# Normalising the attention input on ScalarE instead of VectorE, and all query projections ahead of all key projections

## The reference, cut to what matters

```python
x = x + layernorm(attn(layernorm(x), Mq, Mk, Mv))
x = x + layernorm(ffn(layernorm(x), w_gate, w_up, w_down))

def attn(x, Mq, Mk, Mv):        # x: 2048 x 1024 per batch, 8 heads of 64
    q = x @ Mq; k = x @ Mk; v = x @ Mv       # 512, 512, 1024 wide
    ...                                       # softmax over scores, times v
```

## Time and profile before

| what | value |
|---|---|
| median of 8 runs | 2291.67 us (2288.68 to 2415.04) |
| the profiled execution | 2290.75 us |
| its span on the slowest core | 2289.2 us |
| TensorE matmul busy | 1911.4 us (83%) |
| VectorE busy | 780.6 us (34%) |
| ScalarE busy | 872.8 us (38%) |

### The profile page before, as it was taken

The page is one execution under the profiler, slowest core; times in us unless marked ns, Lnnn a source line. Parts: engine busy times, 40 slices in busy tenths (PEclk is TensorE's granted clock), DMA queues, the critical chain, the costliest instruction groups (busy, mean ns, idle before and its releaser), DMA issues. The chain is left out here.

```text
span 2289.2 us, 35866 instructions; the slowest of 8 cores (2280.0 to 2289.2 us)
## 1 busy us (share of the span) xinstructions
PE 1911.4 (83%) x12864; PEld 1044.9 (46%) x12864; DVE 780.6 (34%) x1657; ACT 872.8 (38%) x1528; POOL 187.1 (8%) x150
## 2 busy tenths in 40 slices
PE   2967888886779995999956798888868999779997
PEld 1423565664435442444423345656644444334443
DVE  6123555656222213112125125556562121231211
ACT  2102888875422212211113128878753111131111
POOL 0011000101101011000110000001010000200002
PEclk7989798897789997999977897998987999979999
DMA  7097000000766404121041300000005220112201
GB/s 183 8 161 127 2 2 1 2 2 6 151 158 134 106 38 147 56 74 56 32 127 26 74 1 1 2 1 2 2 7 178 74 74 19 62 68 74 74 19 56
DMA packets 84553, 136.53 MB, mean 60 GB/s; under 512 B 29088, under 2 KB 33184, under 8 KB 84384
## 3 DMA queue, kind: packets, MB, share of 16 engines
q1 hardware_dynamic: 67744, 106.97, 14.6%
q0 software_dynamic: 16640, 27.27, 8.5%
HBM read 121.63 MB, written 35.65 MB: 69 GB/s over the span
## 5 line engine op out<-in xcount | busy, mean ns | idle before, releaser
L579 ACT ACTIVATE att<-S 128x1024 bf16<-128x1024 f32 x512 | 518.9, 1022 | 112.9 <-PE S L500 111.4
L842 PE MATMUL psG<-x2T,wgT 128*128 128x512 bf16 x1536 | 369.9, 384 | 16.4 <-ACT hT L862 16.4
L853 PE MATMUL psU<-x2T,wuT 128*128 128x512 bf16 x1536 | 363.9, 380 | 0.0
L893 PE MATMUL psD<-wdT,hT 128*128 128x512 bf16 x1536 | 332.2, 379 | 5.8 <-PEq L57 5.8
L865 DVE TENSOR_TENSOR hT<-hT,psU 128x512 bf16<-128x512 bf16 x192 | 132.0, 688 | 531.5 <-PE psU L853 518.0
L862 ACT ACTIVATE hT<-psG 128x512 bf16<-128x512 f32 x192 | 114.8, 598 | 491.8 <-PE psG L842 491.7
L461 PE MATMUL O<-v,att 128*128 128x128 bf16 x4096 | 284.6, 229 | 0.0
L461 PEld LDWEIGHTS O<-v,att 128*128 128x128 bf16 x4096 | 248.4, 103 | 48.4 <-issue 48.4
L842 PEld LDWEIGHTS psG<-x2T,wgT 128*128 128x128 bf16 x1536 | 150.8, 99 | 196.0 <-issue 24.2
L893 PEld LDWEIGHTS psD<-wdT,hT 128*128 128x128 bf16 x1536 | 150.0, 98 | 188.0 <-issue 7.7
L853 PEld LDWEIGHTS psU<-x2T,wuT 128*128 128x128 bf16 x1536 | 150.7, 98 | 183.0 <-issue 3.1
(11 more groups left out here) (81 smaller groups left out, 1053.3 us busy)
## 6 DMA issues: line engine op xcount, KB each, us to landing
wgT<-wgT_scratch SPq DMA_DIRECT2D x36, 512.0 KB, 3.5
wuT<-wuT_scratch SPq DMA_DIRECT2D x36, 512.0 KB, 4.3
x_sb<-x SPq DMA_DIRECT2D x8, 2048.0 KB, 11.9
out<-x_sb SPq DMA_DIRECT2D x32, 512.0 KB, 2.6
wdT<-wdT_scratch SPq DMA_DIRECT2D x2, 6144.0 KB, 35.4
xn_stage<-wd POOLq DMA_DIRECT2D x24, 256.0 KB, 5.2
wdT_scratch<-wks SPq DMA_DIRECT2D x24, 256.0 KB, 5.5
wgst<-wg POOLq DMA_DIRECT2D x24, 256.0 KB, 5.0
```

The costliest lines, as they stand in the source:

```text
L579: S.add("scalar", lambda sc, K=K, att_out=att_out, sl6=sl6, c=c: sc.activation(att_out, Sp[K % 2][:, :], AF.Exp, scale=0.125, accum_out=ac ...
L842: S.add("tensor", lambda tt, wsl=wsl, wcol=wcol, dt=dt, gsl=gsl, c2=c2: tt.matmul(psG[gsl][:, :], wgT_s[wsl][:, wcol + 128 * dt:wcol + 128 ...
L853: S.add("tensor", lambda tt, wsl=wsl, wcol=wcol, dt=dt, gsl=gsl, c2=c2: tt.matmul(psU[gsl][:, :], wuT_s[wsl][:, wcol + 128 * dt:wcol + 128 ...
L893: S.add("tensor", lambda tt, slot=slot, tau=tau, d2h=d2h, ht=ht, Sc=Sc: tt.matmul(psD[slot][tau][:, 512 * d2h:512 * (d2h + 1)], hT[:, 1024 ...
```

## The change

The first layer norm's per-tile operation moves from VectorE to ScalarE, as an Identity activation with a bias and a scale for each partition. The bias is now minus mean times reciprocal root, so the small VectorE operation ahead of it becomes two. Within a tile the order on ScalarE is: normalisation, then the copy of the same tile's transposes. The q and k groups are reordered: 16 q groups, then 16 k groups, in each the four row blocks for one quarter of columns. The first half of Mv is loaded after group 16 and the second after group 32, and each quarter of k is copied to `kTs` as soon as its four groups are evacuated.

```diff
-            negm_done = S.add("vector", lambda v, g4=g4, mean_v4=mean_v4: v.tensor_scalar(
-                nmr1[:, 4 * g4:4 * g4 + 4], mean_v4, -1.0, None, AL.mult),
+            nm1_done = S.add("vector", lambda v, g4=g4, mean_v4=mean_v4: v.tensor_tensor(
+                nmr1[:, 4 * g4:4 * g4 + 4], mean_v4, rstd1[:, 4 * g4:4 * g4 + 4], AL.mult),
                 waits=[(c_act, rstd_done)], inc=c_dve)
+            negm_done = S.add("vector", lambda v, g4=g4: v.tensor_scalar(
+                nmr1[:, 4 * g4:4 * g4 + 4], nmr1[:, 4 * g4:4 * g4 + 4], -1.0, None, AL.mult),
+                waits=[(c_dve, nm1_done)], inc=c_dve)
             for t in tiles:
-                S.add("vector", lambda v, t=t: v.tensor_scalar(
+                S.add("scalar", lambda sc, t=t: sc.activation(
                     xn_bf[:, D * (t % 2):D * (t % 2 + 1)], x_sb[:, D * t:D * (t + 1)],
-                    nmr1[:, t:t + 1], rstd1[:, t:t + 1], AL.add, AL.mult),
+                    AF.Identity, bias=nmr1[:, t:t + 1], scale=rstd1[:, t:t + 1]),
                     waits=[(c_dve, negm_done), (s_tp, tp_base + t - 1)], inc=s_xn)
...
-        for c in range(4):
-            for q in range(4):
+        for q in range(4):
+            for c in range(4):
                 proj_groups.append(("q", q, c))
-            for q in range(4):
+        for q in range(4):
+            for c in range(4):
                 proj_groups.append(("k", q, c))
...
-                        waits=[(s_proj, proj_base + 28 + 4 * half)],
+                        waits=[(s_proj, proj_base + 16 * (half + 1))],
...
-                lastg = 28 + i1
-                if lastg % 2 == 0:
-                    kw = [(s_evP, evP_base + lastg // 2 + 1)]
-                else:
-                    kw = [(s_evPA, evPA_base + (lastg + 1) // 2)]
+                kw = [(s_evP, evP_base + 10 + 2 * i1), (s_evPA, evPA_base + 10 + 2 * i1)]
```

## The result

The changed kernel takes 2331.68 us (median of 11 runs, 2326.86 to 2591.07) against 2291.72 us of the kernel before on the same chip (31 runs). The ratio is 1.0173, interval 1.0154 to 1.0192: slower, inside the forecast range. The profiled execution took 2327.58 us (span 2325.9), 36.8 us more than that of before; the sum had said 2323.9. The mean granted clock lies between 0.904 and 0.907 on all eight cores.

The account below looks back on a forecast made before the run. VectorE's statistics and normalisations paced the preparation, and TensorE waited for Mv ahead of v. 2290.75 + 41.6 (normalisation on ScalarE) - 8.5 (Mv loads) = 2323.9 us, range 2311 to 2334.

Parts of the forecast that it names:

- the sum: Whole kernel: 2290.75 us plus 41.6 for the normalisation's move, less 8.5 for the Mv loads, 2323.9 us.
- the trip: First layer norm's preparation: each tile costs a full ScalarE-TensorE round trip without overlap, 3.40 us; +41.6 us in two batches.
- the first leg: Preparation, per tile: start of normalisation on ScalarE to start of TensorE's transposes, 1.39 us of the 3.40 us.
- The other legs: Preparation, per tile: start of transposes to the copy 1.10 us, copy to ScalarE's next normalisation 0.91 us.
- only the dearer operation counts: Rival, preparation: only ScalarE's longer normalisation costs, 1.19 against 0.77 us, 13.4 us more; with the load 2296 us; chance 0.03.
- VectorE relieved: Rival, preparation: copies don't hold back normalisations, ScalarE sets the pace at 9.6 us a group; 2275 us; chance 0.04.
- Transposes at 2.4 GHz: Rival, preparation: transposes at the higher clock take some 0.4 us off each of 32 tiles, 13 us; 2311 us; chance 0.05.
- Table loads: Rival, preparation: Identity needs its own table, two loads of 1.28 us a group add 20.5 us; 2344 us; chance 0.02.
- Part 2, the loads: Ahead of v: reordered q and k and earlier Mv loads shorten TensorE's wait, -8.5 us in two batches, bounds -15.9 to -5.3.
- the one value of 13.0 us for both batches: Ahead of v: TensorE's wait for Mv's second half, about 13.0 us a batch; 26.0 against 34.5 us before.
- 11.4 to 12.1 us: Ahead of v: reckoned end of Mv's second-half load, its remaining 0.48 MB moving at 150 to 195 GB/s.
- 1.6 on top: Ahead of v: 1.6 us added because the same reckoning for Mv's first half before ended that much short of its matmul.

Follow-up runs that it names:

- the best version: Kernel before, next four tiles' preparation laid between q and k groups, x's second half behind Mk (batch one), Mv into free buffers (batch two): 2257.34 us, ratio 0.985.

## Why the prediction was right

**Part 1, the trip.** Right in mechanism, short by 3.3 us (+41.6 against +44.9). The mis-sized term is the first leg, "start of the normalisation to start of the transposes 1.39 us". I read it from the first trip of a group in the FFN, and it is the exception: the next trip of the same stretch goes from the normalisation of 910.72 to the transposes of 912.21, the middle row of before shown above, in 1.49 us. The changed stage shows that tile after tile (1216.66 to 1218.15, 1220.16 to 1221.66; 28 of its 32 trips are 1.49 or 1.50 us). Sixteen tiles by 0.10 us are 1.6 us a batch, which is nearly all of it. The other legs held: 1.11 and 0.90 us for 1.10 and 0.91.

**That the order in the list decides.** Shown by one run: with the same operations on the same engines in another order the stretch takes 39.8 us instead of 59.7. The rival "only the dearer operation counts" (2296 us) falls with it, and so does "VectorE relieved" (2275 us): even with the overlap restored the two parts together come to 2287.4 us, no gain, since ScalarE, which also has the copies, takes VectorE's place as the pacemaker at 10.24 us a group, not the 9.6 of that rival. The Trainium skill, "Perfetto Trace Analysis", section Optimizing Scalar/DVE Operations, says that offloading some work of a saturated DVE to Scalar may make sense. VectorE was 80% busy here, and the move lost some 49 us in one order and 7.4 us in the other, so it did not pay in this stage.

**Transposes at 2.4 GHz.** In batch two the clock was granted at 0.50, the 1.2 GHz level, as reckoned, and eight transposes took 1.01 us. In the first group of batch one they took 1.01 us too (4.05 us for 32); the 1.00 that the table prints there is no grant on record (last section). So this bound of the prediction, 0.4 us a tile by the earlier trace rows, was not to be had in this stage.

**Table loads.** None: 32 instructions more on ScalarE are the 32 normalisations.

**Part 2, the loads.** -8.5 us were reckoned and -9.9 measured, within the bounds. The wait came in one piece of 10 to 12 us, and the run with the late k copies shows that they had slowed the load. The mis-sized term is the one value of 13.0 us for both batches: it was 13.3 and 11.3. (The prediction's own terms, 11.4 to 12.1 us and 1.6 on top, give 13.0 to 13.7; it took the lower end.) The DMA issues behind the two loads differ in one respect, in after from 138.3 to 142 us and from 1332.8 to 1336.5 us:

```profile
wpg<-mv POOLq DMA_DIRECT2D x1, 1024.0 KB, 12.4
kTs<-kT SPq DMA_DIRECT2D x2, 256.0 KB, 7.4
xn_stage<-wd POOLq DMA_DIRECT2D x2, 256.0 KB, 13.3
```

```profile
wpg<-mv POOLq DMA_DIRECT2D x1, 1024.0 KB, 10.5
kTs<-kT SPq DMA_DIRECT2D x2, 256.0 KB, 6.8
```

In batch one two loads of down weights share GpSimd's queue with Mv; batch two has none. But they do not settle it. All eight cores issue them, and in this execution four of the eight have their fifth v matmul 10.1 to 10.7 us behind the load's issue in batch one, within the 9.9 to 11.2 us of batch two; the other four need 11.0 to 12.6, the slowest core most. Why the load takes longer on some cores in batch one stays open, and no run took the down weights away. The Trainium skill's fit ("DMA: Bandwidth & Descriptors", section Anatomy of one DMA) gave an estimate of 4.4 us for such a load. The four of this core land in 8.8 to 12.4 us, and the one that had the DMA engines to itself in 8.5 us; the trace decides.

**The sum.** 2323.9 us against 2327.58 in the profiled execution: +3.3 from the trip, -1.4 from the loads, and about 2 us that are in neither stage.

## What to carry to other kernels

When an operation moves to another engine, write down that engine's list and ask whether it now holds both the start and the end of a round trip: if the end is queued ahead of the next start, the tiles run one at a time, whatever the double buffers allow, and the fix is one line's place. Then count all that the new engine does per tile, since a relieved engine gains only what the next pacemaker leaves. And take a leg of a trip from its steady repetition in the trace, not from the first one after a wait.

## What the runs showed that I had not expected

The windows table's clock has to be held against other rows. From 21.00 to 36.06 us it prints 1.00, yet eight transposes took 1.01 us there, the same as at 0.50. But the trace's clock entries for this core begin only at 83.9 us, and ahead of the first one the table prints 1.00 for want of an entry. TensorE's own rows speak for the lower level until then. Up to 83.82 us its weight loads for the projections start 0.43 us apart, as they do in batch two until the grant of 0.50 ends at 1278.5 us, and from there 29 of them take 6.17 us, 0.21 each (timeline of after):

```profile
82.97 0.15 PEld L385 LDWEIGHTS psP<-xnT,wpg 128*128 128x128 bf16 x1 [0.28 <-issue]
83.40 0.15 PEld L385 LDWEIGHTS psP<-xnT,wpg 128*128 128x128 bf16 x1 [0.28 <-issue]
83.82 6.17 PEld L385 LDWEIGHTS psP<-xnT,wpg 128*128 128x128 bf16 x29 [0.28 <-issue]
```

Where entries exist, the transposes go with the clock. In the best version, laid between projection groups of a stretch that is granted 1.00, eight of them take 0.61 us (its windows table and its timeline):

```profile
1202.85:1221.54 18.69, 15.81 (x96) 7.98 (x96) 11.26 (x22) 6.61 (x10) 0.75 (x1) 1.00 0.04 4
```

```profile
1204.87 0.61 PE L265 MATMUL pstp<-ident,xn_stage 128*128 128x128 bf16 x8 [0.91 <-DVE xn_stage L258]
```

So a 1.00 at the start of a trace proves nothing about the clock there; look for rows whose pace is known at both levels.
